# Two attention layers on one core: how the negated row maxima of layer 1 reach the Q stack

## The reference

```python
xn = layer_norm(x, norm_w, norm_b)
q = (xn @ q_w + q_b).reshape(8, 512, 16, 32)
k = (xn @ k_w + k_b).reshape(8, 512, 16, 32)
att = einsum('bnhl,bmhl->bnmh', q, k) + (1 - mask) * -1e6
att = softmax(att, axis=2)                 # over the keys m
v = ((xn @ v_w + v_b) * src_mask).reshape(8, 512, 16, 32)
y = einsum('bnmh,bmhl->bnhl', att, v).reshape(8, 512, 512)
e = silu(emb) @ emb_w + emb_b              # scale and shift
h = layer_norm(y, ...) * (1 + scale) + shift
return x + silu(h) @ out_w + out_b
```

## Time and profile before

| | us |
|---|---|
| median of 3 runs | 1376.7 |
| lowest, highest run | 1375.37, 1378.49 |
| profiled execution, first to last instruction (span) | 1373.9 |
| PE busy | 1333.1 (97%) |
| PE's weight load busy | 1059.5 (77%) |
| DVE busy | 1014.5 (74%) |
| ACT busy | 782.5 (57%) |
| POOL busy | 747.4 (54%) |
| DMA queue of SP, share of 16 engines | 42.3% |

### The profile page before, as it was taken

The page is one execution under the profiler, slowest core; times in us unless marked ns, Lnnn a source line. Parts: engine busy times, 40 slices in busy tenths (PEclk is TensorE's granted clock), DMA queues, the critical chain, the costliest instruction groups (busy, mean ns, idle before and its releaser), DMA issues.

```text
span 1373.9 us, 28281 instructions
## 1 busy us (share of the span) xinstructions
PE 1333.1 (97%) x10936; PEld 1059.5 (77%) x10936; DVE 1014.5 (74%) x2004; ACT 782.5 (57%) x1357; POOL 747.4 (54%) x674
## 2 busy tenths in 40 slices
PE   8999999999999899999999999999999999999998
PEld 5778888888888787677777777777777777777666
DVE  5887978788787877678757857857857856856855
ACT  5455455454545563756756755765765765765663
POOL 0323243432333433548947957956966965965832
PEclk9999999999999999999999999999999999999999
DMA  9011111312113356846546546556456456454512
GB/s 340 35 43 62 39 64 37 100 31 70 62 39 93 93 184 200 246 124 185 160 118 178 154 132 178 143 143 177 135 152 172 129 156 161 140 153 140 157 30 93
DMA packets 83303, 173.44 MB, mean 126 GB/s; under 512 B 7624, under 2 KB 7624, under 8 KB 83168
## 3 DMA queue, kind: packets, MB, share of 16 engines
q1 hardware_dynamic: 83168, 171.62, 42.3%
HBM read 104.45 MB, written 67.14 MB: 125 GB/s over the span
## 4 chain that ended last, share of the span: by engine, by line
PE 71%; DVE 13%; ACT 7%; DMA 3%; SPq 2%; issue 2%; POOL 1%; DVEq 0%; ACTq 0%
PE ps L546 13%; PE ps L548 12%; PE ps L547 12%; PE ps L722 8%; PE ps L775 8%; PE ps L705 8%; DVE cT L1253 4%; PE ps L541 4%; PE ps L727 2%; ACT Qs L963 2%; ACT xTh L835 2%; ACT ps L837 2%; DVE ps L1220 1%; PE ps L655 1%; PE ps L634 1%
## 5 line engine op out<-in xcount | busy, mean ns | idle before, releaser
L1441 POOL TENSOR_TENSOR Pb<-Pb 128x512 f32<-128x512 f32 x360 | 449.9, 1291 | 209.5 <-PE ps L775 209.3
L1253 DVE TENSOR_REDUCE cT<-ps 128x1 f32<-128x512 f32 x512 | 324.4, 681 | 110.9 <-PE ps L705 108.6
L986 ACT ACTIVATE Pb<-ps 128x512 f32<-128x512 f32 x512 | 285.3, 600 | 210.8 <-PE ps L722 203.5
L722 PE MATMUL ps<-Qs,Ks 106*128 106x512 f32 x512 | 197.1, 419 | 6.4 <-DVE xTl L1105 3.3
L705 PE MATMUL ps<-Ks,Qs 98*128 98x512 f32 x512 | 185.2, 413 | 4.1 <-DMA Ks<-stack_scratch 1.0
L1365 POOL TENSOR_TENSOR rs<-ve,mhalf 128x4 f32<-128x4 f32 x32 | 33.0, 1031 | 216.9 <-DVE ve L1073 158.4
L722 PEld LDWEIGHTS ps<-Qs,Ks 106*128 106x128 f32 x512 | 95.5, 189 | 52.2 <-issue 12.4
L705 PEld LDWEIGHTS ps<-Ks,Qs 98*128 98x128 f32 x512 | 96.9, 191 | 47.0 <-DVE cT L1253 15.5
L546 PE MATMUL ps<-xTh,Wh_k 128*128 128x512 f32 x256 | 106.9, 418 | 5.9 <-DVE xTl L1105 3.0
L546 PE MATMUL ps<-Wh_o,sTh 128*128 128x512 f32 x256 | 106.8, 417 | 2.1 <-DVE sTl L1231 2.1
L546 PE MATMUL ps<-Wh_v,xTh 128*128 128x512 f32 x256 | 103.1, 403 | 0.0
(11 more groups left out here) (180 smaller groups left out, 2968.1 us busy)
## 6 DMA issues: line engine op xcount, KB each, us to landing
Qs<-stack_scratch SPq DMA_DIRECT2D x32, 768.0 KB
Ks<-stack_scratch SPq DMA_DIRECT2D x32, 768.0 KB
stack_scratch<-sg_q SPq DMA_DIRECT2D x32, 512.0 KB, 2.7
stack_scratch<-sg_k SPq DMA_DIRECT2D x32, 512.0 KB, 2.7
wr<-in_x SPq DMA_DIRECT2D x32, 256.0 KB, 4.8
x_scratch<-wr SPq DMA_DIRECT2D x32, 256.0 KB, 2.0
stack_scratch<-sg_q SPq DMA_DIRECT2D x32, 256.0 KB, 3.1
stack_scratch<-sg_k SPq DMA_DIRECT2D x32, 256.0 KB, 3.4
```

The lines of the kernel that those rows point to most:

```text
L722: e.matmul(bank[:], Ks[par][0:RE, j, m * 128:(m + 1) * 128], Qs[par][0:RE, j, :], start=True, stop=True).then_inc(s["ST"], 1)
L986: e.activation(p_buf(n, m)[:, j, :], ps[bank_of["a", n, m, j]][:], ACT.Exp).then_inc(s["P"], 1)
L1253: e.tensor_reduce(nx[:, n % 2, j, t, 0:1], ps[bank_of["S", n, j, t]][:], AX.X, ALU.max, negate=True).then_inc(s["S_max"], 1)
L1441: e.tensor_tensor(acc[:, j, :], acc[:, j, :], p_buf(n, m)[:, j, :], ALU.add).then_inc(s["Ps_pool"], 1)
```

## The change

The maxima are turned by DVE instead of PE, and put into the stack by DMA instead of ACT. `nxs` becomes 128 x 4 x 32 (per token tile 4 high parts, 4 low parts and 24 columns of zeros). After the three reductions DVE transposes all of `nxs`, 128x128, in blocks of 32x32 into `nxT` in SBUF. Then SP issues eight small DMAs from SBUF to SBUF: for each of four blocks of 32 tokens and for the high and the low part, 4 partitions x 4 tiles x 32 numbers of `nxT` (2 KB in pieces of 128 B) go to one row (98 or 99) of `Qs[n % 2]`, each head to its own columns. `RE` falls from 106 to 100, and the rows of `Ks` from 98 on are ones, set once by POOL. The four matmuls, their PSUM bank, the two ACT casts, `kpick` and `kset` go. The marks in `PLAN` of nearly every part of layer 1's steps are new. In the new marks `nxt` stands at the end of its step, DVE's part first and SP's eight DMAs after it.

```diff
-RM, RX, RE = 96, 98, 106
+RM, RX, RE = 96, 98, 100
-    "S": (0.216,), "nxt": (1.2, 0.3, 0.0),
+    "S": (0.216,), "nxt": (1.2, 0.0),
-    "att": ((0.154, 0.267, 0.392, 0.584, 0.736), (0.002, 0.187, 0.345, 0.514, 0.66), (0, 0.298, 0.519, 0.672, 0.873), (0, 0.275, 0.306, 0.45, 0.581)),
-    "pv": ((0.365, 0.753, 0.853), (0.338, 0.788, 0.924), (0.466, 1.021, 1.054), (0.328, 0.788, 0.957)),
+    "att": ((0.23, 0.282, 0.342, 0.597, 0.635), (0.115, 0.165, 0.223, 0.472, 0.541), (0.129, 0.166, 0.403, 0.559, 0.679), (0.211, 0.252, 0.355, 0.426, 0.448)),
+    "pv": ((0.367, 0.773, 0.859), (0.344, 0.718, 0.978), (0.378, 0.937, 0.947), (0.336, 1.125, 1.14)),
-    "S": ((0.405, 0.414, 0.494, 0.654, 0.71), (0.151, 0.37, 0.491, 0.614, 0.834), (0.186, 0.206, 0.601, 0.645, 0.677), (0.211, 0.351, 0.417, 0.515, 0.783)),
-    "nxt": ((0.859, 0.967), (0.899, 0.931), (0.862, 0.895), (0.743, 1.188)),
-    "q": ((0.053, 0.264, 0.375), (0, 0, 0.02), (0.052, 0.151, 0.265), (0, 0.014, 0.449)),
-    "k": ((0.339, 0.496, 0.539), (0, 0.001, 0.269), (0.13, 0.286, 0.316), (0.161, 0.264, 0.33)),
-    "stack": ((0.734, 0.734), (0.534, 0.534), (0.847, 0.847), (0.717, 0.717)),
+    "S": ((0.439, 0.453, 0.569, 0.684, 0.689), (0.314, 0.398, 0.579, 0.85, 0.949), (0.051, 0.203, 0.667, 0.92, 1.2), (0.141, 0.335, 0.376, 0.484, 0.951)),
+    "nxt": ((1.03, 1.101), (1.065, 1.165), (1.166, 1.176), (1.123, 1.191)),
+    "q": ((0.039, 0.293, 0.429), (0, 0, 0), (0.021, 0.092, 0.13), (0.003, 0.057, 0.097)),
+    "k": ((0.481, 0.532, 0.575), (0, 0, 0.002), (0.022, 0.153, 0.345), (0.075, 0.217, 0.328)),
+    "stack": ((1.015, 1.127), (0.298, 0.542), (0.766, 1.2), (0.347, 0.871)),
...
@@ tensor
-            def nxt(i, n):
-                if i == 1:
-                    bank = take(("nxt", n))
-                    e.wait_ge(s["nx_lo"], n + 1)
-                    for t in range(NT):
-                        r = e.matmul(bank[0:RE, t * 128:(t + 1) * 128], nxs[:, 10 * t:10 * t + RE], identr[:],
-                                     start=True, stop=True)
-                    r.then_inc(s["nx_tr"], 1)
-                if m == 0 and j % 2 == 0:
-                    e.wait_ge(s["nxq"], 2 * n + 1 + j // 2)
+                if m == 0 and j == 0:
+                    e.wait_ge(s[f"nxq{par}"], 128 * (n // 2 + 1))
@@ scalar
-                if i == 2:
-                    rows = ps[bank_of["nxt", n]][RM:RE, :].unsqueeze(1).to_broadcast([RE - RM, 2, T])
-                    e.wait_ge(s["nx_tr"], n + 1)
-                    for h in range(2):
-                        e.copy(Qs[n % 2][RM:RE, 2 * h:2 * h + 2, :], rows).then_inc(s["nxq"], 1)
@@ vector, nxt, after the three reductions
+                    if n:
+                        e.wait_ge(s[f"nxq{(n - 1) % 2}"], 128 * ((n - 1) // 2 + 1))
+                    e.wait_ge(s["nx_lo"], n + 1)
+                    e.transpose(nxT[:], nxs[:].rearrange("p t c -> p (t c)").bitcast(F32)).then_inc(s["nx_tr"], 1)
@@ gpsimd, once
+                    e.memset(Ks[p][RM:RM + 32].bitcast(F32), 1.0).then_inc(s["k_set"], 1)
@@ sync
+            def nxt(i, n):
+                if i == 1:
+                    par = n % 2
+                    if n >= 2:
+                        e.wait_ge(s["ST"], 16 * (n - 1))
+                    else:
+                        e.wait_ge(s["q_set"], 2)
+                    e.wait_ge(s["nx_tr"], n + 1)
+                    for u in range(4):
+                        for r in range(2):
+                            row = Qs[par][RX + r:RX + r + 1, :, :].rearrange("p j (t n) -> p j t n", t=NT)[:, :, :, 32 * u:32 * u + 32]
+                            src = nxT[32 * u + 4 * r:32 * u + 4 * r + 4, :].rearrange("j (t n) -> j t n", t=NT)
+                            e.dma_start(row.bitcast(F32), src).then_inc(s[f"nxq{par}"], 16)
...
-    nc = bacc.Bacc("TRN2", target_bir_lowering=False, num_devices=1)
+    nc = bacc.Bacc("TRN2", target_bir_lowering=False, num_devices=1, dynamic_dma_scratch_size=4096)
```

More of the change, by code:

```diff
@@ L33 @@
     "qk": MM + (0.3, 0.0), "stack": (0.0,), "lx": (0.0,), "lr": (0.0,),
-    "S": (0.216,), "nxt": (1.2, 0.3, 0.0),
+    "S": (0.216,), "nxt": (1.2, 0.0),
     "a": (0.216,), "pv": (2.0,), "den": (0.9,), "dl": (2.0,), "ae": (0.0,),
     "tl": (0.3,), "tle": (0.5, 0.5), "tlx": (0.1, 0.3, 0.4, 0.4, 0.4, 0.4),
-    "stacks": (0.0,), "kset": (0.5, 0.5), "ones": (0.0,), "ahead": (0.0,), "narrow": (0.0,), "end": (0.0,),
+    "stacks": (0.0,), "ones": (0.0,), "ahead": (0.0,), "narrow": (0.0,), "end": (0.0,),
 }
@@ L70 @@
     "zty": ((0, 0.688, 0.728), (0, 0.915, 1.019), (0, 0.954, 1.105), (2, 0, 0.2), (2, 1.0, 1.15)),
[L71 to L75, removed]
+    "zS": ((0.197, 0.481, 0.592, 0.694, 0.896), (0.409, 0.79, 1.107, 1.192, 1.2), (0.168, 0.299, 0.533, 0.643, 0.942), (0.251, 0.439, 0.669, 0.902, 0.999)),
+    "znxt": ((0.935, 1.028), (1.2, 1.2), (0.954, 1.149), (0.323, 0.884)),
+    "zq": ((0.1, 0.239, 0.403), (0.024, 0.182, 0.21), (0, 0.054, 0.807), (0.34, 0.793, 1.029)),
+    "zk": ((0.361, 0.402, 0.405), (0.242, 0.317, 0.523), (1.168, 1.2, 1.2), (0.291, 0.451, 0.797)),
+    "zstack": ((0.44, 1.018), (0.68, 1.2), (0.045, 0.629), (0.979, 1.2)),
     "tle": (None, None, None, (0.3, 0.45)),
@@ L150, in the_order @@
               [("qk", 1, 0), ("qk", 1, 1), ("stack", 1)], [("ny", B - 1)], tiles("v", 8), [("ty", B - 1, c) for c in range(5)],
-              tiles("o", B - 1), max_parts(0) + [("nxt", 0)], [("kset",)],
+              tiles("o", B - 1), max_parts(0) + [("nxt", 0)],
               [("sta", B - 1)])
@@ L249, in bank_uses @@
         return [p], [p]
-    if k == "nxt":
-        return [("nxt", p[1])] if i == 1 else [], [("nxt", p[1])] if i == 2 else []
     return [], []
@@ L331, in cond_two_layers @@
         pick = sb("pick", [128, B])
-        kpick = sb("kpick", [128, 4])
         cU = sb("cU", [128, 8, B])
@@ L342, in cond_two_layers @@
         nx = cT[:].rearrange("p a b -> p (a b)").rearrange("p (n j t s) -> p n j t s", n=2, j=4, s=2)
-        nxs = sb("nxs", [128, RM + 10 * NT], FR)
+        nxs = sb("nxs", [128, NT, 32], FR)
+        nxT = sb("nxT", [128, NT * 32])
         identr = sb("identr", [128, 128], FR)
@@ L461, in done @@
                 return s["S_max"], 16 * key[1] + 4 * key[2] + key[3] + 1
-            if k == "nxt":
-                return s["nxq"], 2 * key[1] + 2
             return s["P"], 16 * key[1] + 4 * key[2] + key[3] + 1
@@ L784, in _ @@
             parts = {"m": m, "mb": mb, "tx": tx, "k": k, "v": v, "te": te, "q": q, "st": state, "y": y, "ty": ty, "o": o,
-                     "qk": qk, "S": S, "nxt": nxt, "a": a, "pv": pv, "den": den, "dl": dl}
+                     "qk": qk, "S": S, "a": a, "pv": pv, "den": den, "dl": dl}
             for p, i in order:
@@ L988, in _ @@
             parts = {"w": w, "nx": nx_, "ny": ny, "tx": tx, "k": k, "te": te, "v": v, "q": q, "sta": sta, "y": y, "ty": ty,
-                     "early": early, "kset": kset, "qk": qk, "nxt": nxt, "a": a}
+                     "early": early, "qk": qk, "a": a}
             for p, i in order:
@@ L1257, in nxt @@
                 if i == 0:
-                    w = nxs[:, RM:].rearrange("p (t c) -> p t c", c=10)
                     m = nx[:, n % 2].rearrange("p j t s -> p t j s")
-                    hi = w[:, :, 2:6]
+                    hi = nxs[:, :, 0:4]
                     if n:
@@ L1263, in nxt @@
                     else:
-                        e.wait_ge(s["nx_set"], 3)
+                        e.wait_ge(s["nx_set"], 2)
                     e.wait_ge(s["S_max"], 16 * n + 16)
@@ L1270, in nxt @@
                     with nc.allow_low_precision(reason="the sum of a number and its negated high part is exact"):
-                        e.tensor_reduce(w[:, :, 6:10], m, AX.X, ALU.add).then_inc(s["nx_lo"], 1)
+                        e.tensor_reduce(nxs[:, :, 4:8], m, AX.X, ALU.add).then_inc(s["nx_lo"], 1)
+                    if n:
+                        e.wait_ge(s[f"nxq{(n - 1) % 2}"], 128 * ((n - 1) // 2 + 1))
+                    e.wait_ge(s["nx_lo"], n + 1)
+                    e.transpose(nxT[:], nxs[:].rearrange("p t c -> p (t c)").bitcast(F32)).then_inc(s["nx_tr"], 1)
             def tl(i, n):
@@ L1356, in prologue @@
                 e.wait_ge(s["sel"], 2)
[L1357 to L1361, removed]
             def scales(kind, p, x):
@@ L1643, in _ @@
             parts = {"w": w, "m": m, "tx": tx, "k": k, "ty": ty, "o": o, "ahead": ahead, "stacks": stacks, "narrow": narrow, "qk": qk,
-                     "stack": stack, "lx": lx, "lr": lr, "end": end}
+                     "stack": stack, "nxt": nxt, "lx": lx, "lr": lr, "end": end}
             for p, i in order:
```

17 lines of the change are left out of this document (5 added, 12 removed), and 2 rows, old and new, of the table PLAN.

## The result

The changed kernel takes 1538.55 us (median of 4, 1534.59 to 1540.2) against 1376.23 (median of 4, 1375.37 to 1378.49): ratio 1.1167 (95% interval 1.1133 to 1.1202), 162 us slower. The forecast was 1401, its range up to 1428: the sign was right, the size far off.

A forecast was written before the change was run, and what follows sets the result against it. PE, 97% busy, was taken to bound the kernel. DMA waits of +49.8 less 12.5, 5.1 and 8 gave +24.2 on the profiled 1373.9, 1398.1; with the median 2.8 over that span, 1401 us, range 1354 to 1428.

The forecast's parts named there:

- What bounds the kernel: Whole kernel: time is PE's list plus its gaps, 5.9 us a sequence, some 47 in all.
- step 1: PE: four products a step leave its list, 0.39 us x 32, all on the path: -12.5 us.
- step 2: PE: its waits for the small reductions go: -5.1 us.
- step 3: ACT and PSUM banks: relief from 64 fewer casts and one customer less, -8 us, bounds 0 and 35.
- Step 4: DVE: an added 128x128 transpose of 0.32 us a step, 10 us in all, hides except in the chain.
- Step 5, T and the covers: Last `S` to first `a`: when the transpose ends (T) and how long PE's list covers, leaving 2.35 to 3.3 us spare.
- Step 5, the length of the chain: Transpose end to last DMA's landing (c): 4.2 us, bounds 3.1 and 5.9; PE's waits beyond the spare add 49.8 us.
- Step 6: SP's queue: eight issues a step take 97 us in all, delaying nothing wanted soon: 0 us.
- rival C: SP's queue: the eight DMAs stand behind the stack's loads and land later, +36 us, 1437 us; chance 0.12.
- A: New chain: the eight DMAs go out nearly together and are covered, 1351 us; turning point c = 3.4; chance 0.27.
- B: PE's gaps: waits come, but the gaps of 47 us shrink with them, relief 30 instead of 8, 1379 us; chance 0.13.
- The signs I had named: Profile after: right if PE idles before most first `a`, about 2 us each; wrong if under 0.85 us a step in the mean.

The follow-up runs named there:

- e11: Changed kernel without any small DMAs (`a` waits for the transpose, maxima left out), with the marks of the kernel before: 1345.86 us, 0.9792.
- e10: Changed kernel without any small DMAs (`a` waits for the transpose, maxima left out), at the new marks: 1342.37 us, 0.9757.
- e3: Kernel before (products on PE, casts on ACT) with the new marks: 1436.85 us, 1.0441.
- e1: Changed kernel with only the first of the eight small DMAs of a step, maxima left out of most columns: 1346.65 us, 0.9789.
- e12: Changed kernel with the high part of the maxima alone, four DMAs a step instead of eight, new marks; a repeat run: 1378.99 us, 1.0033.
- e7: Changed kernel with the four high-part DMAs issued by SP and the four low-part ones by ACT: 1425.54 us, 1.0348.
- e5: Changed kernel with the high part alone (four DMAs a step) and the marks of the kernel before: 1496.34 us, 1.0859.
- e8: Changed kernel with the high part alone, two of its four DMAs issued by SP and two by ACT: 1358.65 us, 0.9872.
- e9: Kernel of e1 with five groups of eight 2 KB DMAs of different shapes behind its last store; a single execution, time not compared.
- e6: Changed kernel with 14 discarded matmuls of 512 columns on PE before each step's wait for the eight DMAs: 1471.79 us, 1.0706.

## Why the prediction was wrong

**What bounds the kernel: right.** PE's list and its gaps. Work taken off PE, step 1 (12.5), waits, step 2 (5.1), and relief, step 3 (8), were 25.6 together; e11 has 29.2, e10 32.7. The three aren't told apart by any run; if steps 1 and 2 stand, relief is 11.6 by the old marks, inside its bounds and above the 8.

**Step 4 (transpose hidden): right.** 311 ns each, 10.0 us; with the old marks DVE goes from 1014.5 to 1024.4 (e11). That it is 1037.4 after is the new marks' doing (with them the old mechanism has 1027.1, e3) and isn't on the path, since e10 (1035.9) is the fastest kernel.

**Step 5, T and the covers: right.** T was to be 5.2, 7.5, 5.4, 3.55 and is 4.8, 7.7, 5.4, 3.0; the covers were to be 7.7, 9.9, 8.7, 5.9 and are 7.3, 9.7, 8.5, 5.5. Counting PE's list against DVE's works to half a microsecond. That holds for steps 4 to 27; in the last two I gave no cover, and e1's trace has 2.8 and 2.2 us there.

**Step 5, the length of the chain: this failed, in its issue term.** I took seven distances of 0.38 from the mask's small DMA; they are 0.67. That is 2.0 of the 2.3 us by which c is longer (6.5, over my upper bound of 5.9); the landing, 1.68 for 1.4, is most of the rest. The row was of a DMA from HBM to SBUF, the new ones go from SBUF to SBUF, and no such DMA stood in the trace. (The 0.66 of the load beside it in the earlier trace rows is the longest of its line's 28; their median is 0.43.) I widened the bounds for the landing from that doubt and not for the issue (0.47 at most), though the issue counts seven times. With 6.5 the waits are 4.0, 4.5, 3.4, 4.0 a sequence, 15.9 x 8 = 127 for the 127.4 measured. My own sum would have gone from +49.8 to about +121 (2.3 more in each of 31 steps) and the forecast to 1472.

**A missing term: the clock.** This is the second thing that failed: the sum has no term for it. The rest, 1538 less 1472, is 66 us, and the clock's 70.6 us above account for it. I wrote that PE's granted clock is 1.00 in every step and took 0.235 us a matmul as given. I named who would run dry behind the waiting `a` (ACT and POOL, rightly: 0.00 us of work in the 3.9 us window) and not that PE's own pace would fall after the wait: 2.2 us a step on top of some 4 of waiting. In e12 the waits are 1.0 us a step in the mean and the clock is 0.987; in e7 1.9 and 0.974; in the kernel after 4.0 and 0.929.

The Trainium skill has this in "TensorE: Matmul & The Clock Gate", section "HAM oscillation — how this bites in real kernels": a matmul loop that waits for a DMA in each turn starts every turn at the low clock, so the cost is paid once a turn. This trace agrees for 29 of the 32 steps, with 6.1 us at 0.54 in the one shown; behind the three shortest waits PE didn't start at the low clock.

**Step 6 (SP's queue): right that it costs nothing, wrong in its size.** The issues take 32 x 5.35 = 171 us of the queue and not 97. PE doesn't wait longer for what stands behind them: `S` waits 3.0 us in all for the stack loads, both in the kernel after and in e1 with one small DMA. That what stands before them can matter so much (e5) I had as rival C.

**The rivals.** *A* (covered, 1351) described e1 and e10 (1347, 1342) and its turning point, c = 3.4, held with e12: 1379 with c = 0.1 + 3 x 0.67 + 1.7 = 3.8, its T 0.43 shorter by two reductions, is about no change. There is some luck in that: the gains are 33 us and not 25.6, the waits 31.7 and not 25, and the clock, which I had left out, takes 6. *B*: PE's idle time beside the wait for the DMAs is 1536.7 - 1379.5 - 127.4 = 29.8 us after and 1344.5 - 1308.9 = 35.6 in e10's profiled execution: while PE waits the other gaps shrink by 6, not by another 22. *C*: the mechanism is real, in the old marks, and absent in the new ones, as the "against" said.

The sentence of the Trainium skill that I weighed under A ("DMA: Bandwidth & Descriptors", section "Issuing engines are not separate DMA queues"), that the time to initiate a DMA "is usually small relative to the DMA itself", doesn't hold for these small DMAs: one takes 0.62 us of SP and lands 1.68 us after its start, and eight issues take 5.35 us. The same sentence says that issuing on several engines saves only the sequencer's time; here that is much: 113 us with four on each engine (e7) and 20 with two (e8 beside e12).

**The signs I had named.** PE idle before the first `a`, released by the DMA into `Qs`: yes. "About 2 us each": 4. "Over 4 in the last two": 3.7 and 4.3. "SP's eight issues take 2.6 to 3.0": 5.35. The last lands within 1 to 2: 1.7. ACT near 720: 717. DVE 10 more: 23, of which the transposes are 10.

## What to carry to other kernels

A DMA's issue is time of the engine that issues it, and in a chain with several of them it counts once for each: take its price from a DMA with the same two ends, and if there is none, give that term the widest bounds, since it is multiplied. A wait of about 4 us in a full TensorE cost half as much again by the slower clock behind it; waits of 1 us a step cost little. Price the matmuls behind a long wait at the lower level as well. What helped here: fewer issues (four DMAs in place of eight, and two small reductions less, took 160 us off), spread over two engines, and none shortly behind a large load in the same queue.

## What the runs showed of the hardware

- An issue of a 2 KB DMA from SBUF to SBUF holds the issuing queue 0.57 to 0.63 us on SP (medians; 0.62 to 0.67 from start to start, 0.67 in the kernel's own shape) and 0.64 to 0.67 on ACT; pieces of 128 B, 512 B or 2 KB change it by 0.06 at most (e9). From SBUF to HBM it is 0.34 from start to start (e9), from HBM to SBUF 0.38 for the mask's 16 KB.
- Such a DMA lands 1.7 us after its issue starts when no load stands shortly before it (kernel after), and 3.8 to 7.2 when it goes out shortly behind 1.5 MB of loads (e5).
- After 3.9 us without work the granted clock was 0.54 over 6.1 us of work. 14 discarded matmuls in the place of each wait kept it at 0.992 in the mean and made the kernel 67 us faster (e6).
